# Attention layers: own rows join the weighed rows on VectorE, ScalarE weighs gathered rows three pairs ahead; the convolution gathers by pairs

## The reference

```
xw    = x @ W
xj    = xw[src] + edge_emb;  xi = xw[dst]
alpha = leaky_relu(att_i . xi + att_j . xj)
alpha = exp(alpha - max over dst) / sum over dst
out   = mean over heads of segment_sum(xj * alpha, dst) + b
```

## Time and profile before

| | before |
|---|---|
| median of 3 runs (lowest to highest) | 5821.73 us (5819.69 to 5822.21) |
| profiled execution | 5835.43 us, of it the span 5833.6 us |
| mean granted TensorE clock | 0.88 |
| busy share of the span, PE / DVE / ACT / POOL | 83% / 71% / 56% / 52% |
| the five attention layers | from about 1700 to 3790 us of the span |
| the convolution pass | from about 4775 to 5110 us |

### The profile page before, as it was taken

How to read it: one execution, slowest core, us unless ns; L and a number is a source line. 1 busy time by engine, 2 the same in 40 slices (tenths; PEclk the granted TensorE clock), 3 DMA queues, 4 the chain that set the end, 5 groups by cost and what they waited for, 6 DMA issues and landing times. The chain is left out here.

```text
span 5833.6 us, 104695 instructions
## 1 busy us (share of the span) xinstructions
PE 4824.4 (83%) x29899; PEld 4142.3 (71%) x29899; DVE 4143.7 (71%) x15589; ACT 3247.3 (56%) x8537; POOL 3035.7 (52%) x2871
## 2 busy tenths in 40 slices
PE   4999999999959969969969969866995767868666
PEld 3777777777749959959969959844774656746565
DVE  4677777778867668767767768786676667847765
ACT  1777877877736636636636636543772336746500
POOL 0666666655575445445355356222651347555367
PEclk6999999999979979979979979955997778989855
DMA  2999986665545535535535435388663447845332
GB/s 69 167 216 209 210 210 209 210 203 195 192 116 128 123 77 130 117 83 127 111 89 130 104 98 134 87 244 227 151 147 79 138 132 207 233 110 114 66 92 86
DMA packets 1111146, 841.29 MB, mean 144 GB/s; under 512 B 210522, under 2 KB 1063102, under 8 KB 1110256
## 3 DMA queue, kind: packets, MB, share of 16 engines
q1 hardware_dynamic: 1030276, 706.02, 47.0%
q0 software_dynamic: 77040, 128.08, 10.5%
q10 hardware_dynamic: 3264, 0.50, 0.1%
HBM read 390.57 MB, written 448.11 MB: 144 GB/s over the span
## 5 line engine op out<-in xcount | busy, mean ns | idle before, releaser
L747 POOL DMA_INDIRECT gat_G<-table,k_src_row x980 | 1030.8, 1052 | 629.2 <-PE gat_psE L1523 422.5
L1520 PE MATMUL gat_psG<-gat_ends_at,gat_Gw 128*128 128x128 f32 x3920 | 718.5, 279 | 12.3 <-DVE gat_loop L1317 12.3
L1520 PEld LDWEIGHTS gat_psG<-gat_ends_at,gat_Gw 128*128 128x128 f32 x3920 | 599.9, 193 | 15.5 <-issue 12.8
L451 POOL TENSOR_TENSOR nodes_rstd<-nodes_var,k_half 128x14 f32<-128x14 f32 x138 | 360.4, 2612 | 398.1 <-DVE nodes_var L511 390.8
L1521 PE MATMUL gat_psG<-k_ident,gat_loop 128*128 128x128 f32 x1960 | 538.2, 275 | 0.0
L1446 ACT ACTIVATE gat_aggT<-gat_psG 128x512 f32<-128x512 f32 x490 | 292.5, 597 | 396.8 <-PE gat_psE L1523 396.8
L1534 PE MATMUL gat_psZ<-gat_aggT,t_gat_wh 128*128 128x256 f32 x1960 | 504.8, 380 | 1.3 <-ACT gat_hT L1453 1.3
L1523 PE MATMUL gat_psE<-gat_ends_at,gat_wex 128*128 128x128 f32 x1960 | 381.9, 277 | 0.0
L1453 ACT ACTIVATE gat_hT<-gat_psZ,t_gat_bias 128x256 f32<-128x256 f32 x490 | 232.0, 473 | 240.8 <-PE gat_psZ L1535 240.8
L1438 ACT ACTIVATE gat_loop<-gat_own,gat_al 128x128 f32<-128x128 f32 x980 | 335.0, 392 | 49.8 <-DVE gat_al L1291 49.8
L1534 PEld LDWEIGHTS gat_psZ<-gat_aggT,t_gat_wh 128*128 128x128 f32 x1960 | 335.4, 191 | 27.9 <-issue 2.1
(11 more groups left out here) (652 smaller groups left out, 14598.8 us busy)
## 6 DMA issues: line engine op xcount, KB each, us to landing
table<-nodes_rows SPq DMA_DIRECT2D x660, 198.0 KB
table<-nodes_n SPq DMA_DIRECT2D x396, 192.0 KB
gat_own<-table SPq DMA_DIRECT2D x490, 132.0 KB
table<-gat_rows SPq DMA_DIRECT2D x392, 132.0 KB
nodes_x<-in_x SPq DMA_DIRECT2D x132, 192.0 KB
out<-nodes_x_out SPq DMA_DIRECT2D x132, 192.0 KB
gat_ex<-in_ex_pad SPq DMA_DIRECT2D x70, 336.0 KB
gat_G<-table,k_src_row POOLq DMA_INDIRECT x980
```

The source lines that it names most:

```text
L451: eng.tensor_tensor(rstd[:, k % 3, :], var[:, k % 3, :], K.half[:, 0:M], ALU.pow).then_inc(s.pow, 1)
L747: eng.indirect_dma_start(to, None, table, bass.IndirectOffsetOnAxis(ap=index, axis=0)).then_inc(sem, 16)
L1520: eng.matmul(o[:, h * P:(h + 1) * P], Gw[:, i % RS, t, h, :], ends_at[:, i % RS, t, :], start=True, stop=False)
```

## The change

In the attention layers:

- The identity matmuls of `loop` (line 1521) and the tile `loop` go. The own row, times its weight, is added to `Gw` before the aggregation: the own weight is zero but at the last edge of a run, where `ends_at` keeps the place.
- Weighing the gathered rows (`Gw`) moves from one VectorE operation per pair to four ScalarE ones (`weigh`), issued three pairs ahead of the eviction: weigh(i+3) at the end of iteration i, but none at k = 4 and two at k = 5, since the next group's weights come then.
- VectorE adds own rows with four fused multiply-adds (scalar_tensor_tensor) in place in `Gw`, after waiting for `weighed`. TensorE waits for `looped` alone.
- The rings of `ends_at` and `Gw` grow from 4 to 6.
- Except for the first group (`late`), the steps for the next group move: source_scores to k = 0 (from 3), turn_scores to 0 (from 1), scores to 3 (from 4), exp to 3 (from 4), weights to 5 (from 6), turn_weights to 4 (from 5). take_weights stays at 6.

In the convolution the ring of 20 tiles is counted in pairs (GS 2, RG 10 for 4 and 5), the second gather of a pair also waits for `mixed` of eleven pairs back, and power(b) is asked for after every pair.

```diff
 table, first, w = (K.gat_out, 0, D) if last else (K.tables[l + 1], K.rows, ROWW)
-RG, RS, RO, RR, RA = 3, 4, 6, 5, 4
+RG, RS, RO, RR, RA = 3, 6, 6, 5, 4
 AHEAD = 2 * PG + 3
...
 ex, wex = A.sb("ex", [P, 2, GM, 3 * EDGE_F]), A.sb("wex", [P, 2, GM, P])
-ends_at, Gw, loop = A.sb("ends_at", [P, RS, 2, P]), A.sb("Gw", [P, RS, 2, H, P]), A.sb("loop", [P, RS, 2, H, P])
+ends_at, Gw = A.sb("ends_at", [P, RS, 2, P]), A.sb("Gw", [P, RS, 2, H, P])
 aggT, aggE = A.sb("aggT", [P, RA, 2, H, P]), A.sb("aggE", [P, RA, 2, P])
...
     "seq", "fill_out", "fill_in", "ox_in", "sq", "scores_turned", "step", "to_exp", "exped", "alphas", "alphas_turned", "al",
-    "weighed", "wex", "loop1", "loop0", "agg", "aggT", "aggE", "mixed", "hT", "rowed", "rows_done", "pieces", "sc", "st_in",
+    "weighed", "wex", "looped", "agg", "aggT", "aggE", "mixed", "hT", "rowed", "rows_done", "pieces", "sc", "st_in",
     "weights", "weights_turned", "wc", "px", "pe", "pie_turned", "pieE_turned", "pr", "prE", "comb", "summed", "aggX", "zx",
...
     return g // ring + 1
+
+def late(g):
+    return int(g == 0)
...
             if i >= RO:
-                eng.wait_ge(s.loop0, i - RO + 1)
-                eng.wait_ge(s.loop1, i - RO + 1)
+                eng.wait_ge(s.looped, i - RO + 1)
             eng.dma_start(own[:, i % RO, :, :], rows_of(K.tables[l], K.rows, i)).then_inc(own_in[i % RO], 16)
...
             if g >= 2:
-                eng.wait_ge(s.loop0, PG * (g - 1))
+                eng.wait_ge(s.weighed, PG * (g - 1))
             eng.tensor_copy(al[:, g % 2, :, :], psT[:, 3 * P:3 * P + 2 * LN].rearrange("p (k a) -> p k a", k=2)).then_inc(s.al, 1)
...
                               ALU.is_equal)
-            a = al[:, g % 2, 0, :].rearrange("p (h t) -> p t h", h=H)[:, 2 * k:2 * k + 2, :]
-            eng.tensor_tensor(Gw[:, i % RS, :, :, :], spread(G[:, g % RG, 2 * k:2 * k + 2, 0:D], 2, H), spread(a, 3, D), ALU.mult
-                              ).then_inc(s.weighed, 1)
+            eng.wait_ge(s.weighed, i + 1)
             eng.wait_ge(own_in[i % RO], 16 * uses(i, RO))
             for t in range(2):
-                a = GM + 2 * k + t
-                ins = eng.tensor_scalar(loop[:, i % RS, t, 1, :], own[:, i % RO, t, 0:D], al[:, g % 2, 1, a:a + 1], None, ALU.mult)
-            ins.then_inc(s.loop1, 1)
+                for h in range(H):
+                    a = h * GM + 2 * k + t
+                    ins = eng.scalar_tensor_tensor(Gw[:, i % RS, t, h, :], own[:, i % RO, t, 0:D], al[:, g % 2, 1, a:a + 1],
+                                                   Gw[:, i % RS, t, h, :], ALU.mult, ALU.add)
+            ins.then_inc(s.looped, 1)
...
             if i < NP and g + 1 < NG:
-                if k == 3:
+                if k == (3 if g == 0 else 0):
                     source_scores(g + 1)
-                if k == 4:
+                if k == 3 + late(g):
                     scores(g + 1)
+                if k == PG - 2 + late(g):
+                    weights(g + 1)
                 if k == PG - 1:
-                    weights(g + 1)
                     take_weights(g + 1)
...
-        def own_loop(i):
+        def weigh(i):
             g, k = divmod(i, PG)
             eng.wait_ge(s.al, g + 1)
-            eng.wait_ge(own_in[i % RO], 16 * uses(i, RO))
+            eng.wait_ge(g_in[g % RG], 16 * GM * uses(g, RG))
             if i >= RS:
...
             for t in range(2):
-                a = 2 * k + t
-                ins = eng.activation(loop[:, i % RS, t, 0, :], own[:, i % RO, t, 0:D], ACT.Copy, scale=al[:, g % 2, 1, a:a + 1])
-            ins.then_inc(s.loop0, 1)
+                for h in range(H):
+                    a = h * GM + 2 * k + t
+                    ins = eng.activation(Gw[:, i % RS, t, h, :], G[:, g % RG, 2 * k + t, 0:D], ACT.Copy, scale=al[:, g % 2, 0, a:a + 1])
+            ins.then_inc(s.weighed, 1)
...
         exp(0)
-        own_loop(0)
-        own_loop(1)
+        for i in range(3):
+            weigh(i)
         for i in range(NP + 2):
...
                 to_rows(i - 2)
-            if i < NP and k == 4 and g + 1 < NG:
+            if i < NP and k == 3 + late(g) and g + 1 < NG:
                 exp(g + 1)
-            if i + 2 < NP:
-                own_loop(i + 2)
+            if i + 2 < NP and k == 5:
+                weigh(i + 2)
+            if i + 3 < NP and k != 4:
+                weigh(i + 3)
         eng.wait_ge(s.zx, 1)
...
             g, k = divmod(i, PG)
-            eng.wait_ge(s.weighed, i + 1)
-            eng.wait_ge(s.loop1, i + 1)
-            eng.wait_ge(s.loop0, i + 1)
+            eng.wait_ge(s.looped, i + 1)
             if k == 0:
...
                 for h in range(H):
-                    eng.matmul(o[:, h * P:(h + 1) * P], Gw[:, i % RS, t, h, :], ends_at[:, i % RS, t, :], start=True, stop=False)
-                    eng.matmul(o[:, h * P:(h + 1) * P], loop[:, i % RS, t, h, :], K.ident[:, :], is_transpose=True,
-                               start=False, stop=True)
+                    eng.matmul(o[:, h * P:(h + 1) * P], Gw[:, i % RS, t, h, :], ends_at[:, i % RS, t, :], start=True, stop=True)
                 mm = eng.matmul(psE[i % 2][:, t * P:(t + 1) * P], wex[:, g % 2, c, :], ends_at[:, i % RS, t, :],
...
                 aggregate(i)
-            if i < NP and g + 1 < NG and k == 1:
+            if i < NP and g + 1 < NG and k == late(g):
                 turn_scores(g + 1)
...
                 to_rows(i - 2)
-            if i < NP and g + 1 < NG and k == 5:
+            if i < NP and g + 1 < NG and k == 4 + late(g):
                 turn_weights(g + 1)
...
 NP, SI = C // 2, CAT_TYPES * CAT_S
-GS, RG, RZ, RK, RB, RX = 4, 5, 5, 9, 7, 18
+GS, RG, RZ, RK, RB, RX = 2, 10, 5, 9, 7, 18
 NB = C // (2 * RB)
...
                 c = g * GS + t
-                if t % 2 == 0 and c >= RG * GS:
-                    eng.wait_ge(s.gr, (c - RG * GS) // 2 + 1)
+                if t == 0 and g >= RG:
+                    eng.wait_ge(s.gr, g - RG + 1)
+                if t == 1 and g > RG:
+                    eng.wait_ge(s.mixed, g - RG)
                 gather(eng, K.tables[6], K.src_row[:, c:c + 1], G[:, g % RG, t, :], g_in[g % RG])
-            if 2 * g >= RB * (done + 1) + NORM:
+            if g >= RB * (done + 1) + NORM:
                 power(done)
...
         def relu(i):
-            g, k = divmod(i, 2)
-            eng.wait_ge(g_in[g % RG], 16 * GS * (g // RG + 1))
+            eng.wait_ge(g_in[i % RG], 16 * GS * (i // RG + 1))
             if i >= 3:
                 eng.wait_ge(s.agg, i - 2)
-            eng.activation(gr[:, i % 3, :, :], G[:, g % RG, 2 * k:2 * k + 2, :], ACT.Relu).then_inc(s.gr, 1)
+            eng.activation(gr[:, i % 3, :, :], G[:, i % RG, :, :], ACT.Relu).then_inc(s.gr, 1)
```

## The result

The changed kernel takes 5769.97 us (median of 4 runs, 5764.7 to 5778.86) where the kernel before takes 5821.97 (median of 4, 5819.69 to 5824.38): a ratio of 0.9912, 95% interval 0.9895 to 0.9929, so 52 us faster. The prediction said 5754 in a range of 5690 to 5815. The profiled execution of after has a span of 5766.2 us, 67.4 less than that of before; 11 of these lie in stages that the change doesn't touch and are taken as the scatter between two executions (6 of them before the first attention layer). The rest is 43.8 us in the attention layers and 12.5 in the convolution.

The account below looks back on a forecast made before the run. TensorE bounds by a hair; after the change a relay of ScalarE's weighing, VectorE and TensorE's turn sets each group. Gains of 30 (layers 1 to 4), 31.5 (layer 0) and 6 (convolution), 68 us, give 5754 us, range 5690 to 5815.

Parts of the forecast that it names:

- The bound: Attention layers: a relay between engines sets the group's period, 25.2 us in layers 1 to 4, 23.2 in layer 0.
- some 0.25 for the refilled array and the last result: Estimated part of the 1.9 us that the relay spends on TensorE's turn and aggregation of pair 5.
- The pause: TensorE waits for VectorE at each turn of the weights: 2.8 us in layers 1 to 4, 0.8 in layer 0.
- the 3.65 us of my sum: Relay term: ScalarE's weighing ends 3.65 us after TensorE ends a group's first pair.
- Layers 1 to 4: 11 x 0.55 + 3.5 - 2.0 = 7.5, four times: Attention layers 1 to 4: eleven shorter intervals, free last pairs, less the join; 30 us gained in all.
- The ends of a layer: Each attention layer: nothing for the first two groups, 3.5 us gained by eight free last pairs, 2.0 lost at the join.
- The join of the runs: End of each attention layer: VectorE's scans start after pair 97's multiply-adds and the exponential comes later, costing 2.0 us.
- The convolution: Convolution pass: earlier powers shorten VectorE's waits; 6 us gained, between a gain of 15 and a loss of 3.
- TensorE as the bound: Rival, attention layers: VectorE has the weights 2.8 us sooner, so TensorE sets the pace; 42 us a layer, 5604 us, chance 0.10.
- No overlap of the multiply-adds: Rival, VectorE in the attention layers: multiply-adds take 0.34 us each; 48 us of gain lost, 5802 us, chance 0.07.
- The falling clock: Rival, attention layers: TensorE's pauses of 2.8 us a group lower its clock; decides from 1.2 us a group, chance 0.06.
- a clock under 1.00 inside a layer: Sign in the profile after: TensorE's granted clock below 1.00 in an attention layer would make the forecast wrong.

Follow-up runs that it names:

- The added passes: The changed kernel plus twelve needless identity passes per group on TensorE: at pairs 1, 2, 3 5789.56 us; at pairs 5, 6, 0 5845.61 us.
- the look-ahead of two: The changed kernel with ScalarE weighing pair i+2 instead of i+3 at the end of iteration i, from the second group on: 5988.44 us, ratio 1.0281.
- the two kernels: The changed kernel with VectorE's scores behind pair 2: 5898.73 us; the same with exponential and weights also a pair earlier: 5832.55 us.
- the longer look-ahead: The changed kernel with ScalarE weighing one more pair ahead, masks and edge rows asked for two pairs earlier: 6045.59 us, ratio 0.9794.
- the three steps moved: The changed kernel with scores, exponential and weights each a pair earlier from the second group on: 5832.55 us, ratio 1.001.
- after with the old powers: The changed kernel with the convolution's powers asked for where the kernel before asked, behind every second pair: ratio 0.9939.

## Why the prediction was right, and where not

- **The bound.** Right. TensorE 3.08 us a pair, a relay of 25.2 us a group in layers 1 to 3 (25.23), 23.2 in layer 0 (23.13), VectorE's wait of about 1 us at pair 3 (1.08), 0.26 us a multiply-add, 5.9 us of scores. The added passes and the look-ahead of two show that the relay is a cause and not only a fit: each moved the period of layers 1 to 3 by what the sum says (1.31 us for 1.32, and 28.45 for 28.3 in the groups that run shortest). The term "some 0.25 for the refilled array and the last result" was called an estimate and had no row, and no run shows it by itself; turn to eviction, of which it is a part, takes 1.87 us (2221.29 to 2223.16) for the forecast's 1.9: 0.23 to the start of the aggregation, 1.44 for it, and 0.20 more to the eviction's start.
- **The pause.** 2.8 us a group in all, as forecast for layers 1 to 3, but in two halves: 1.37 at the turn and 1.17 at pair 4, which I had not seen. The multiply-adds of pair 4 stand behind the scores; they end 8.74 us after pair 3's began (2207.77 to 2215.39 + 1.12), and with the 3.65 us of my sum that is 12.4 us after TensorE's aggregation of pair 0, whereas TensorE wants them at 4 x 3.08 less its aggregation of 1.34 and plus 0.33 for the turned scores, 11.3 us. The total is fixed by the relay, so the time came out right; the split matters for the clock. In layer 0 it is 0.70 for the forecast's 0.8.
- **Layer 4: the step that failed.** "Layers 1 to 4: 11 x 0.55 + 3.5 - 2.0 = 7.5, four times" took the old period of layer 4 as 25.75. It was 24.50: its rows are two plain transposes and it has no scores to copy, and TensorE waited there for the weights already:

```profile
3441.64 0.30 PE L1503 MATMUL gat_psT<-k_ident,gat_alB 28*128 28x28 f32 x2 [0.66 <-DVE gat_alB L1285]
...
3466.14 0.30 PE L1503 MATMUL gat_psT<-k_ident,gat_alB 28*128 28x28 f32 x2 [0.63 <-DVE gat_alB L1285]
```

  The new relay's period is 24.76. I read one layer's group and multiplied by four. The forecast's gain of 7.5 us became a loss of 4.4, 12 us of the error.
- **The ends of a layer.** I took the first two groups as no gain and the end as 3.5 - 2.0 = 1.5. The "cold TensorE" of the first groups is a granted clock of 0.50 from 2130 to 2140 us and 0.89 from 2140 to 2150, at the start of layer 1 in the trace of before. The two guesses missed what moving the turn from k = 5 to 4 does: the second interval has six pairs (22.16 for 25.23, a pair's 3.08 less), and nine pairs instead of eight follow the last turn (27.7 us against 28.2, so 0.4 gained, not 3.5). The first interval is 1.4 longer. The join of the runs was sized at 2.0: TensorE's wait for it went from 1.33 to 4.05 us, 2.7. So what follows the last turn grew by 2.3 to 2.4 us, and layer 1 gives 5.7 + 2.2 - 2.4 = 5.5. That layer 0 came out at 32.8 for 31.5 is partly luck: its second interval gave 5.7 where 2 were taken for the first two, and its end lost 2.3 where 1.5 were to be gained.

```profile
2458.45 0.39 PE L1573 MATMUL gat_psT<-k_ident,gat_wt 2*128 2x2 f32 x2 [4.05 <-DVE gat_aself L1363]
```

- **The convolution.** 6 us forecast in a range of -15 to +3; 9 measured alone (4 to 15), 12.5 between the two main traces, 7 to 13 over all. The first power comes 4.8 us earlier, as said, but VectorE's first wait for it shrank less (22.2 to 20.4), and GpSimd reaches its last gather 7.7 us earlier (274.0 us after the first, for 281.7): powers asked at the right pair no longer hold up gathers, and the wait for the ReLU fell from 15.5 to 6.6 us.
- **The total.** 61.5 forecast in the layers, 43.8 found; 6 and 12.5. On the medians 68 and 52. The layers fell short by 17.7 us, the convolution gave 6.5 more than forecast, so the two errors partly cancel.
- **The rivals.** TensorE as the bound (5604; its terms give 5606) is out: in layers 1 to 3, 1.32 us more work at pairs 1, 2 and 3 moves the period by 0.05. No overlap of the multiply-adds (5802) is out by their 0.26 us pace. The falling clock did not happen in layers 0 to 3 once they had started (1.00), where the pauses are 0.70 us, and 1.17 and 1.37. In layer 4, with 1.85 and 1.46 us, the granted clock fell in 5 of 12 groups (0.97 over the stretch): the prediction's sign "a clock under 1.00 inside a layer" did show there, but it cost little, intervals at most 0.2 us longer. The falling clock came true in three of the experiments, with pauses of 2.2 to 4.3 us at one place. In the trace of before the granted clock was 0.50 for 3.4 us (4927.40 to 4930.80) right behind the convolution's pause of 4.44 us, and 1.00 from 4330 to 4350 us, around the pause of 1.97 us:

```profile
4927.40:4930.80 3.40, 3.40 (x14) 3.06 (x13) 3.37 (x18) 0.79 (x3) 2.25 (x3) 0.50 0.86 238
```

## What to carry to other kernels

When work leaves the engine that bounds, ask which relay between engines sets the end of a group, and sum it; the gain is the old period less that sum, not the work that left. Take the old period from each stage that the sum is multiplied by: one layer of five that differs turned a gain into a loss here. Shortening a relay at what its first step waits for (weigh earlier, load earlier) gave 1.2 us a group here. Moving its long step earlier asks two things first: is everything that the step reads there by then, and how long does the engine that wants the work behind it stand? Here the scores found no masks, TensorE's pause grew to 2.2 us and more, its granted clock fell to 0.50 in 46 and in 32 of 48 groups, and the two kernels took 129 and 63 us more than after.

## What the hardware showed that I had not expected

- How often TensorE's granted clock fell, by the pauses in a group, counted from a layer's second turn of the weights on. With 1.17 and 1.37 us in a group (after, layers 1 to 3) it fell in none of 36. With 1.85 (once 2.05) and 1.46 (after, layer 4) it fell in 5 of 12, with 1.86 and 1.37 (the look-ahead of two, layer 0) in 4 of 12, with 1.46 alone (the longer look-ahead, layer 4) in none of 12. With one pause of 2.16 to 2.68 us (the three steps moved) it fell in 14 of 30, with one of 2.78 us or more in all 18, and in all 48 with 4.1 to 4.3 (the look-ahead of two, layers 1 to 4). The fall doesn't always come at once: behind eight of the 18 pauses the first four matmuls still took 0.71 or 0.72 us. Two pauses of 1.17 and 1.37 us were cheaper for the clock than one of about their sum.
- The same kernel took 5822 to 5827 us in some runs and 6171 to 6178 in others, 6% more, while the period of a group hardly differs (25.23 us in after, 25.27 in after with the old powers, run among the slow ones). The difference lies in stages where transfers count: from 400 to 800 us of the span 210 GB/s were moved in the first and 183 in the second, and the first interval of each attention layer takes 38 to 41 us for 26 to 27. Why isn't shown. The texts above speak of a slower chip, but the record numbers the chips of the 5827 us and of the 6178 us both as 8, and that of the 6171 us as 5, so it may as well be something else that was different then.

```profile
400.00:800.00 400.00, 376.43 (x2395) 300.69 (x2394) 310.34 (x1249) 317.22 (x797) 265.41 (x209) 1.00 0.90 210
```

```profile
400.00:800.00 400.00, 347.50 (x2093) 262.88 (x2093) 274.86 (x1098) 278.38 (x697) 233.75 (x184) 1.00 0.78 183
```

The first line is of after, the second of after with the old powers.
